# Attention stages: later transposes, one value product per head pair, an output ring, V rows first

## The reference, cut to what matters

```python
h = _layernorm(x, ln1)
x = x + _attn(h, h)          # 16 heads, keys and values: the 512 positions
h = _layernorm(x, ln2)
x = x + _attn(h, context)    # 16 heads, keys and values: the 64 positions
h = _layernorm(x, ln3)
x = x + feed_forward(h)
# _attn: softmax(q k^T * scale) v for each head, then the output projection
```

## Time and profile before

| | us |
|---|---|
| Runs shown, median (lowest to highest) | 5767.12 (5765.01 to 5771.17) |
| Profiled execution, own time | 5772.53 |
| Its span, first to last instruction | 5770.7 |
| TensorE busy in the span | 5049.1 (87%) |
| VectorE busy | 3934.4 (68%) |
| GpSimd busy | 2549.6 (44%) |
| ScalarE busy | 2275.0 (39%) |

### The profile page before, as it was taken

How to read it: one execution, slowest core, us unless ns; L and a number is a source line. 1 busy time by engine, 2 the same in 40 slices (tenths; PEclk the granted TensorE clock), 3 DMA queues, 4 the chain that set the end, 5 groups by cost and what they waited for, 6 DMA issues and landing times.

```text
span 5770.7 us, 53704 instructions
## 1 busy us (share of the span) xinstructions
PE 5049.1 (87%) x18992; PEld 2658.1 (46%) x18992; DVE 3934.4 (68%) x3924; ACT 2275.0 (39%) x3972; POOL 2549.6 (44%) x1292
## 2 busy tenths in 40 slices
PE   6888888888888888669998799999978999999889
PEld 3445555455555555334444444444444444444444
DVE  2999999999999999946665515555454155554541
ACT  4555545555555554324343223333322133333221
POOL 1555555555555555527773004666400056664000
PEclk8999999999999999879999899999999999999999
DMA  2334433444344344310001000000101000001000
GB/s 82 139 141 142 145 135 136 144 144 143 141 142 146 141 145 140 133 46 1 1 1 37 26 11 1 1 1 1 44 1 37 0 1 1 1 1 44 1 0 15
DMA packets 94440, 376.70 MB, mean 65 GB/s; under 512 B 13025, under 2 KB 14433, under 8 KB 91233
## 3 DMA queue, kind: packets, MB, share of 16 engines
q1 hardware_dynamic: 94176, 373.26, 18.3%
HBM read 369.94 MB, written 3.28 MB: 65 GB/s over the span
## 4 chain that ended last, share of the span: by engine, by line
PE 45%; DVE 6%; POOL 2%; ACT 2%; issue 1%; DMA 0%; SPq 0%; ACTq 0%; DVEq 0%
PE PS L1010 6%; PE PS L1020 6%; PE PS L1034 6%; PE PS L989 5%; PE PS L1176 5%; PE PS L1185 3%; PE PS L1142 3%; PE PS L998 3%; PE PS L1044 2%; POOL PA L957 2%; PE PS L1116 2%; PE PS L1125 1%; DVE CST L1476 1%; DVE PA L1478 1%; PE PS L968 1%; DVE PA L1489 1%
## 5 line engine op out<-in xcount | busy, mean ns | idle before, releaser
L561 POOL TENSOR_TENSOR UH<-UH,BC 128x1152 f32<-128x1152 f32 x512 | 1343.0, 2623 | 1124.4 <-DVE U L620 1124.4
L957 POOL TENSOR_SCALAR PA<-PA,INV 128x512 f32<-128x512 f32 x768 | 1188.5, 1563 | 1296.5 <-DVE INV L1408 1296.5
L357 PE MATMUL Y<-UH,ident_sb 128*128 128x512 f32 (+1 forms) x3072 | 1180.1, 528 | 262.9 <-POOL UH L561 211.4
L628 DVE TENSOR_TENSOR_SCAN UH<-DA,U 128x1152 f32<-128x1152 f32 x512 | 1307.2, 2553 | 21.2 <-ACT DA L507 3.8
L357 PEld LDWEIGHTS Y<-UH,ident_sb 128*128 128x128 f32 x3072 | 593.0, 203 | 891.2 <-issue 571.2
L507 ACT ACTIVATE DA<-DT,NEGA 128x575 f32<-128x575 f32 x1024 | 722.9, 764 | 484.8 <-DVEq L612 259.9
L1247 ACT ACTIVATE PA<-PS,NMX 128x512 f32<-128x512 f32 x768 | 520.4, 682 | 981.4 <-DVE NMX L1402 968.5
L620 DVE TENSOR_TENSOR U<-DTX,BC 128x1152 f32<-128x1152 f32 x512 | 701.5, 1370 | 60.3 <-DVE stream L642 8.0
L1402 DVE TENSOR_REDUCE NMX<-PS 128x2 f32<-128x1024 f32 x384 | 468.0, 1219 | 296.4 <-PE PS L1010 296.4
L1417 DVE COPY VP<-PS 128x512 f32<-128x512 f32 x768 | 491.8, 681 | 15.0 <-PE PS L1020 14.6
L1020 PEld LDWEIGHTS PS<-ident_sb,PA 128*128 128x128 f32 x3072 | 329.4, 142 | 317.0 <-issue 214.7
(11 more groups left out here) (124 smaller groups left out, 5249.3 us busy)
## 6 DMA issues: line engine op xcount, KB each, us to landing
BC<-bc_rows SPq DMA_DIRECT2D x512, 576.0 KB, 3.7
WA<-mamba_a SPq DMA_DIRECT2D x16, 1421.0 KB, 7.4
W<-pair_w SPq DMA_DIRECT2D x6, 3072.0 KB, 10.6
WB<-mamba_b SPq DMA_DIRECT2D x16, 514.0 KB, 5.0
VP<-ff_w SPq DMA_DIRECT2D x2, 3072.0 KB
WO<-out_w SPq DMA_DIRECT2D x4, 1024.0 KB
stream<-x_t SPq DMA_DIRECT2D x2, 1024.0 KB, 6.7
VP<-ff_w SPq DMA_DIRECT2D x2, 1024.0 KB
```

The lines of the kernel that those rows point to most:

```text
L357: mm = pe.matmul(Y[:, a:b], IDENT[:, :], UH[:, SLOT[j], a:b], start=(s == 0), stop=(s == DS - 1), skip_group_check=True)
L561: pool.tensor_tensor(h, h, BC[:, j % NBB, 1, :].unsqueeze(1).broadcast_to([P, HK, T]), ALU.mult).then_inc(s_hc, 1)
L628: dve.tensor_tensor_scan(UH[:, SLOT[j], :], DA[:, j % NDA, :], U[:, 0:HC], 0.0, ALU.mult, ALU.add).then_inc(s_scan, 1)
L957: pool.tensor_scalar(PR[:, n % 3, j, :], PR[:, n % 3, j, :], INV[:, n % 4, j:j + 1], None, ALU.mult).then_inc(s_ps, 1)
```

## The change

It does five things. (1) Cross attention: `turn` and `turned` move from pair at-2 to at-3, `values` and `output` from at-3 to at-4, and TensorE's values now stand behind the scores; the loops are a step longer, the output products and adds one step later. (2) Self attention: `values(it)` comes once for a pair, over all its 512 queries, in step 1 of the next; PT's two buffers hold a whole pair each, so VP grows from 8192 to 12288 columns. (3) ATT becomes a ring of 12 tiles. (4) `value_rows` goes ahead of scores and transposes in step 3, on TensorE and on ScalarE. (5) `finish` goes ahead of its step's transposes, and VectorE's `add` into step 2 behind `shift`. The counts of s_pv halve everywhere. The diff, cut where it only renumbers ATT's or s_pv's indices:

```diff
@@ -691,6 +691,7 @@
 HW = tuple(P // h for h in HPT)
 NTL = tuple(NH // h for h in HPT)
 PPT = tuple(h // 2 for h in HPT)
+NAT = 12
 ALLT = tuple(NB * t for t in NTL)
 TBASE = tuple(sum(ALLT[:l]) for l in range(NT + 1))
 
...
@@ -750,12 +751,12 @@
         W = sb("W", [P, NP, KD, 3, P])
         WO = sb("WO", [P, 2, O_COLS])
         HN = sb("HN2", [P, KD, NB * S0])
-        ATT = sb("ATT", [P, 2, NTL[1], S0])
+        ATT = sb("ATT", [P, NAT, S0])
         KB = sb("KB", [P, NP, NB, P])
         VB = sb("VB", [P, NB, NP, P])
-        VP = sb("VP", [P, 8192])
+        VP = sb("VP", [P, 12288])
         VT = VP[:, 0:4096].rearrange("p (g r c) -> p g r c", g=2, r=QT)
-        PT = VP[:, 4096:8192].rearrange("p (h t j q) -> p h t j q", h=2, t=QT, j=2)
+        PT = VP[:, 4096:12288].rearrange("p (h t j q) -> p h t j q", h=2, t=QT, j=2)
         WFF = VP[:, 0:F_COLS]
         PA = sb("PA", [P, 3072])
         PR = PA[:, :].rearrange("p (n j k) -> p n j k", n=3, j=2)
...
@@ -1021,18 +1022,17 @@
                                                   IDENT[:, :])
                             mm.then_inc(s_tp, 1)
 
-                    def values(it, half):
-                        hh = 2 * it + half
+                    def values(it):
                         tt, t = it // PPT[l], it // PPT[l] % NTL[l]
-                        pe.wait_ge(s_pt, START + 2 * (l * NN + 2 * hh + 2))
+                        pe.wait_ge(s_pt, START + 2 * (l * NN + QT * (it + 1)))
                         pe.wait_ge(s_vn, START + TBASE[l] + tt // QT * QT + QT)
                         pe.wait_ge(s_at, START + TBASE[l] + tt)
                         for kt in range(QT):
                             for j in range(2):
                                 r = row(l, it % NP, j)
                                 c = t % QT * P + r
-                                mm = pe.matmul(PS[r:r + HW[l], B_V, half * 256:(half + 1) * 256],
-                                               VT[:, tt // QT % 2, kt, c:c + HW[l]], PT[:, hh % 2, kt, j, :],
+                                mm = pe.matmul(PS[r:r + HW[l], B_V, :],
+                                               VT[:, tt // QT % 2, kt, c:c + HW[l]], PT[:, it % 2, kt, j, :],
                                                start=(kt == 0), stop=(kt == QT - 1), skip_group_check=True)
                         mm.then_inc(s_pv, 1)
 
...
@@ -1061,20 +1061,18 @@
                             n = it * QT + i
                             if last and tt + 1 < ALLT[l] and i < 2:
                                 project("qk"[i], tt + 1)
+                            if i == 3 and first and tt + QT < ALLT[l]:
+                                value_rows(tt + QT)
                             if n + 2 < NN:
                                 scores(n + 2)
+                            if i == 2 and it >= NP and 1 <= it % NP <= KD:
+                                finish(it // NP - 1, it % NP - 1)
                             if n:
                                 turn(n - 1)
                             if i == 1 and it:
-                                values(it - 1, 1)
-                            if i == 3:
-                                values(it, 0)
-                            if i == 2 and it >= NP and 1 <= it % NP <= KD:
-                                finish(it // NP - 1, it % NP - 1)
-                            if i == 3 and first and tt + QT < ALLT[l]:
-                                value_rows(tt + QT)
+                                values(it - 1)
                     turn(NN - 1)
-                    values(NITS - 1, 1)
+                    values(NITS - 1)
                     for m in range(KD):
                         finish(NB - 1, m)
 
...
@@ -1139,23 +1137,23 @@
                         pe.wait_ge(s_ca, START + TBASE[l] + (b + 1) * NTL[l])
                         pe.wait_ge(s_wo[1], 64 * (l + 1))
                         for t in range(NTL[l]):
-                            mm = pe.matmul(PS[:, 1, :], wo[:, t, m * P:(m + 1) * P], ATT[:, b % 2, t, :],
+                            mm = pe.matmul(PS[:, 1, :], wo[:, t, m * P:(m + 1) * P], ATT[:, (b * NTL[l] + t) % NAT, :],
                                            start=(t == 0), stop=(t == NTL[l] - 1))
                         mm.then_inc(s_op, 1)
 
                     pe.wait_ge(s_rstd, START + (3 * l + 2) * NB)
                     pe.wait_ge(s_cse, START + SBASE[l + 1])
-                    for at in range(NITS + 3):
+                    for at in range(NITS + 4):
                         if at < NITS and at % PPT[l] == 0:
                             query(at // PPT[l])
-                        if 0 <= at - 3:
-                            values(at - 3)
-                        if 0 <= at - 2 < NITS:
-                            turn(at - 2)
+                        if 0 <= at - 3 < NITS:
+                            turn(at - 3)
                         if 0 <= at - 1 < NITS:
                             scores(at - 1)
-                        if NP + 3 <= at < NITS and at % NP in (3, 4):
-                            finish(at // NP - 1, at % NP - 3)
+                        if 0 <= at - 4:
+                            values(at - 4)
+                        if NP + 4 <= at < NITS and at % NP in (4, 5):
+                            finish(at // NP - 1, at % NP - 4)
                     for m in range(KD):
                         finish(NB - 1, m)
 
...
@@ -1302,16 +1300,16 @@
                         tt = it // PPT[l]
                         b, t = tt // NTL[l], tt % NTL[l]
                         act.wait_ge(s_co, START + l * NITS + it + 1)
-                        if b >= 2 and t == 0:
-                            act.wait_ge(s_x, START + l * XADD + NB * KD + (b - 1) * KD)
+                        if tt >= NAT:
+                            act.wait_ge(s_x, START + l * XADD + NB * KD + ((tt - NAT) // NTL[l] + 1) * KD)
                         c = V_BV + NP + t * PPT[l]
-                        act.activation(ATT[:, b % 2, t, :], PS[:, 6 + tt % 2, :], ACT.Identity,
+                        act.activation(ATT[:, tt % NAT, :], PS[:, 6 + tt % 2, :], ACT.Identity,
                                        bias=VEC[:, l % 2, c:c + 1]).then_inc(s_ca, 1)
-                    for at in range(NITS + 3):
-                        if at >= 3 and (at - 3) % PPT[l] == PPT[l] - 1:
-                            output(at - 3)
-                        if 0 <= at - 2 < NITS:
-                            turned(at - 2)
+                    for at in range(NITS + 4):
+                        if 0 <= at - 3 < NITS:
+                            turned(at - 3)
+                        if at >= 4 and (at - 4) % PPT[l] == PPT[l] - 1:
+                            output(at - 4)
                         if 0 <= at - 1 < NITS:
                             exps(at - 1)
 
...
@@ -1409,19 +1407,19 @@
 
                     def copies(n):
                         ng = l * NN + n
-                        hh, i = n // 2, n % 2
+                        it, i = n // QT, n % QT
                         for j in range(2):
                             dve.wait_ge(s_tp, START + 2 * ng + j + 1)
                             if i == 0 and j == 0:
-                                dve.wait_ge(s_pv, START + l * 2 * NITS + max(hh - 1, 0))
-                            dve.tensor_copy(PT[:, hh % 2, :, j, i * P:(i + 1) * P],
+                                dve.wait_ge(s_pv, START + l * NITS + max(it - 1, 0))
+                            dve.tensor_copy(PT[:, it % 2, :, j, i * P:(i + 1) * P],
                                             PS[:, B_T + j, :].rearrange("p (t q) -> p t q", t=QT)).then_inc(s_pt, 1)
 
                     def output(tt):
                         b, t = tt // NTL[l], tt % NTL[l]
                         c = V_BV + t * PPT[l]
-                        dve.wait_ge(s_pv, START + l * 2 * NITS + 2 * (tt + 1) * PPT[l])
-                        dve.tensor_scalar(ATT[:, b % 2, t, :], PS[:, B_V, :], VEC[:, l % 2, c:c + 1], None, ALU.add).then_inc(s_at, 1)
+                        dve.wait_ge(s_pv, START + l * NITS + (tt + 1) * PPT[l])
+                        dve.tensor_scalar(ATT[:, tt % NAT, :], PS[:, B_V, :], VEC[:, l % 2, c:c + 1], None, ALU.add).then_inc(s_at, 1)
 
                     def add(b, m):
                         c = V_BO + m
...
@@ -1442,10 +1440,10 @@
                             inverse(n)
                             if last and tt + 1 < ALLT[l] and i == 0:
                                 query(tt + 1)
-                            if i == 3 and it >= NP and 1 <= it % NP <= KD:
-                                add(it // NP - 1, it % NP - 1)
                             if n + 2 < NN:
                                 shift(n + 2)
+                            if i == 2 and it >= NP and 1 <= it % NP <= KD:
+                                add(it // NP - 1, it % NP - 1)
                             if n:
                                 copies(n - 1)
```

(12 more changed lines are left out.)

## The result

| | before | after |
|---|---|---|
| Median, us (lowest to highest) | 5767.15 (5765.01 to 5771.17) | 5566.74 (5564.04 to 5569.20) |
| Span of the profiled execution, us | 5770.7 | 5567.0 |
| TensorE instructions | 18992 | 17456 |

The ratio is 0.9652, 95% interval 0.9636 to 0.9667.

A forecast was written before the change was run, and what follows sets the result against it. TensorE was taken to bound self attention in layers 2 and 3, GpSimd's run to hold it up in layer 1, an engine loop to bind cross attention. Terms summed to -159 us: 5772.5 to 5613.5, median 5608, range 5582 to 5650.

The forecast's parts named there:

- the sum: All six attention stretches: +11 - 28.5 - 28.5 - 51 - 31 - 31 = -159 us.
- (b): Self attention, layers 2 and 3: two 256-column value products become one of 512, saving 0.15 us a pair.
- It costs nothing in layers 2 and 3: Self attention: output product ahead of the transposes delays VectorE's reciprocal and the scaling, but other TensorE work hides it.
- the pipeline is one step deeper (+4.5): Cross attention, layers 2 and 3: the extra step costs 4.5 us, taken off the 35.6 saved by four batches.
- Both terms of the tile: Layer 1 self attention: query projection to GpSimd's run 15.13 us; run's end to next projection 4.1 us.
- What I had given 3 us: Layer 1 self attention: steps with an output product and the tail add some 3 us to the +7.7.
- (a): Self attention, layers 2 and 3: V rows go first, so a 0.73 us wait goes in 28 of 32 pairs.
- (c): Self attention, layers 2 and 3: the softmax chain gets more time, so the last transposes' wait, some 0.19 us, goes.
- The end: Self attention, layers 2 and 3: the deferred value product makes the tail longer by about 1.7 us.
- The turn: Cross attention: with VectorE's own queue the bound, the period falls from 5.41 to 4.54 us.
- Rival 1: Cross attention: the clock falls all the same, so 25 us of clock stay: 5633 us; chance 0.20.
- Rivals 2 to 4: GpSimd keeps up in layer 1 (0.12, 5584); cross loop stays closed (0.05, 5721); heads' products not side by side (0.03, 5922).

The follow-up runs named there:

- halves_l1: The changed kernel with two half value products per pair again in layer 1's self attention only; 5548.2 us, ratio 0.9614.
- vrows_only: The kernel before with only the V rows moved ahead of step 3's scores and transposes, on TensorE and ScalarE; 5698.8 us, ratio 0.9881.
- vrows_behind: The changed kernel with the V rows moved from the head of step 3 to directly behind step 1's value product; 5591.0 us, ratio 0.9692.
- after_old_fin: The changed kernel with self attention's output product behind the transposes again and VectorE's add ahead of the row maximum; 5576.6 us, ratio 0.9666.
- before_apart: The kernel before with cross attention's two output products two steps apart, adds likewise; 5748.8 us, ratio 0.9968.
- values_ahead: The changed kernel with cross attention's value product ahead of transposes and scores again, transposes still one pair later; 5598.8 us, ratio 0.9706.

## Why the prediction was wrong in size

Of the 41 us that the sum missed, 17 lie in the self attention of layers 2 and 3 and 23 in cross attention. The steps that failed are three: in (b), what a product costs by its neighbours stood at nothing (0.39 us a pair); "It costs nothing in layers 2 and 3", of the output product's place (4 us a layer gained); and "the pipeline is one step deeper (+4.5)", where the ends of the cross stages gained instead.

**Self attention, layer 1** was right in its mechanism, and halves_l1 shows it: the long product holds up GpSimd's run. That the size came out, +11 forecast and +9.8 measured, is luck. The merge costs 22 to 25 us there, and the V rows' move gives 15 back (vrows_only). Both terms of the tile were too long (15.01 for 15.13, 3.83 for 4.1), so a plain tile loses 0.13 us and not 0.52, 1.2 us in the nine of them where I had 7.7 in fifteen. What I had given 3 us made up for it: two tiles with an output product (38.34 us instead of 37.41 each), the last three tiles (4.3 us in all) and the end of the stage, 6.8 us longer from the last query projection on, less 4.4 at the start. The closing value product alone takes 6.53 us there, at half the clock, and 3.63 within the stage.

**Self attention, layers 2 and 3, step (b).** "The columns cost the same; only what is paid once per product goes" was right for the product itself: 3.58 us, a gain of 0.16 against 0.15. The waits of (a) and (c) went as said, 0.73 and 0.23 (forecast 0.19). What failed is that I priced each product by its own length and not by its neighbours. A 128 by 128 product takes some 0.1 us less to the next start behind transposes than behind a value product, and the set of transposes ahead of it 0.1 us less too. The new order puts both the V rows and the query projection behind transposes: 0.18 + 0.10 + 0.10 + 0.10 = 0.48 us a pair. 0.73 + 0.23 + 0.16 + 0.48 = 1.60, which is 18.67 less 17.07. Of the 0.18 for the V rows 0.08 belongs to their wait: V rows behind a value product without a wait take 1.91 (vrows_behind), so the wait had cost 2.72 - 1.91 = 0.81, more than the 0.73 listed. That leaves some 0.39 to the neighbours. vrows_behind takes 0.20 of these back with the same instructions. The Trainium skill's page "TensorEngine Tiling (Array Packing)", section "Key Properties", says that a change of tiling mode drains TensorE. The rows above are in line with it: scores use 64 by 128, value products 128 by 64, transposes and projections 128 by 128, and 0.1 us comes where the shape changes from or to 128 by 128 at these products. But in the kernel before, the query projection takes 1.91 us too, and it stands behind the V rows, a product of its own shape, after a wait. A wait goes with the same 0.1 us, and no run here varied the shape alone, so that it is the drain is argued, not shown. The rows of before had both lengths in view, 1.91 for the query (4761.11 in the earlier trace rows to the scores here) and 1.81 for the key projection:

```profile
4763.02 1.13 PE L1010 MATMUL PS<-QK 64*128 64x512 f32 x4
...
4765.01 1.88 PE L989 MATMUL PS<-HN,W 128*128 128x512 f32 x4
4766.82 1.13 PE L1010 MATMUL PS<-QK 64*128 64x512 f32 x4
```

The 1.60 us come in 21 plain pairs only, 33.6 us. The six pairs with an output product gain 1.02 each, the first pair 4.1, two pairs without V rows 0.9 together. The end, forecast at 1.7 us more, takes 7.2 more from the last query projection on (48.8 to 56.0), of which the first pair's missing half product gives back 1.9: 1.6 of it are the longer products, 3.0 waits for GpSimd and VectorE, and 2.4 the clock of the closing product (6.09 us for 3.65). Every run with the long product has a slow closing product in these layers, 5.1 to 6.6 us.

**The output product's new place**, forecast at nothing, gives 4 us each in layers 2 and 3 (after_old_fin). The forecast had asked only what the product delays behind it, not who waits for its bank: from the old place it is the V rows of the next step, 0.90 us.

**Cross attention.** The loop opened as forecast: VectorE's own queue is the bound. The turn was mis-sized a little, 4.39 us against 4.54: I had added the durations of the multiplication and of the query's evacuation (0.69 and 0.81), where the next instruction starts 0.61 and 0.72 us after them. The output products in the chain of waits of layer 2 (answers to the earlier trace rows):

```profile
4156.98 6.87 PE PS L1140 x16
...
4205.62 6.87 PE PS L1140 x16
...
4291.75 7.12 PE PS L1140 x16
```

A batch is 48.6 us, against 49.2 forecast. In layer 1 it is 38.5 against 37.5, and there 1.7 us of it are clock: where the second product ran fast, as in halves_l1, the batch is 36.8. So four batches save 37.8 us in layer 2 where I had 35.6. The step that failed is the last term: "the pipeline is one step deeper (+4.5)". The deeper pipeline does cost a step at the start: from the first query to the first output product only 4.3 us are saved (60.9 to 56.6) over 11 and 12 steps. But from the last batch's second product to the end 16.1 us are saved (56.4 to 40.3) in six steps and two products, against the 5 or 6 that six turns are worth. There, too, the clock is full after the change: the stage's first closing product takes 7.12 us in the rows above, 9.90 before. TensorE's waits ahead of it were 2.94, 2.69, 0.69 and 0.82 us and are now 1.29, 2.16 and 0.83. I had counted the clock within the batches and charged the depth at the end. Beyond four batches, layers 2 and 3 gained another 2.5 and 0.5 us, and layer 1 6.3 us, where I had charged 4.5, 4.5 and 4.

**The clock.** Rival 1 did not come in layers 2 and 3. The second product of layer 2 after the change:

```profile
4169.06 7.13 PE L1140 MATMUL PS<-ATT,WO 128*128 128x512 f32 x16 [1.31 <-DVE stream L1493]
```

7.13 us after a wait of 1.31 us; the granted clock of the cross stretches is 0.98 and 0.99, before 0.86 and 0.95. In layer 1 it came in part. There the wait for the add is still 2.02 us, and two of the three second products, this one and the next, run at half the clock:

```profile
3186.40 5.40 PE L1140 MATMUL PS<-ATT,WO 128*128 128x512 f32 x8 [2.02 <-DVE stream L1493]
```

The third takes 3.70. Part 4 of the Trainium skill's page "TensorE: Matmul & The Clock Gate" would have the transposes count as idle. After waits of 1.31 us with transposes shortly before, no second product ran slow; at the end of self attention, where only transposes stood between waits of at most 1.67 us, the value product did. The second fits that rule, but no run here took the transposes away alone, so it stays open. That waits bring the low clock is shown in both directions, by before_apart (6.87 us for 8.83 without the wait) and values_ahead (8.83 for 7.13 in two of three batches, with 0.86 us more of it); how long a wait it takes is not fixed by them, as the same 2.17 us gave 8.83 twice and 7.13 once in one kernel.

**Rivals 2 to 4.** GpSimd did not keep up in layer 1, the loop did open, and the heads' products do run side by side.

## What to carry to other kernels

Read what a product costs from the distance between two starts, and read it for each neighbour it can have: the same instructions took 0.2 us less per pair when they stood behind others of their shape. Read the ends of a stage by themselves: here they held more of the error than any pair did. A longer product is no gain where another engine needs the scores behind it; ask for each loop which engine starts late, and choose the length for each layer. A wait on TensorE is paid twice when it lowers the clock: in the kernel before, moving two products a second step apart took 4.1 us off a batch of layer 2 (58.1 to 54.0), 2.17 the wait and 1.96 the clock.

## What the runs showed of the hardware that had not been expected

The low clock is not a fixed answer to an idle time: after the same 2.17 us wait in the same kernel, 16 instructions of 512 columns took 8.83, 7.13 and 8.83 us. A 128 by 128 projection takes 1.81 us to the next start behind transposes and 1.91 to 1.92 behind a value product, or after a wait; a set of eight transposes 0.93 ahead of a 128 by 128 product and 1.02 ahead of scores or a value product. The sixteen instructions of a long value product take 3.65 us within a stage, and 6.09 behind 7.9 us of transposes and waits of at most 1.67 us.
